# Attention scores with the opposite sign, and the masking of heads four to seven split around a scaling

## What is computed

```python
q = _l2norm(q) * q_scale; k = _l2norm(k) * k_scale        # per head, 8 heads of 128
sim = einsum('bhnid,bhnjd->bhnij', qb * 8.0, kw)          # 128 rows x 256 keys
sim = where(mask, sim, finfo.min)                         # causal, two tiles wide
attn = softmax(sim, axis=-1)
o = einsum('bhnij,bhnjd->bhnid', attn, vw) * gates
x = layernorm(x + o @ Wo.T)
```

## Time and profile before

| | |
|---|---|
| median of three runs | 1692.16 us (1691.88 to 1692.72) |
| the profiled execution | 1695.04 us |
| its span, from the first to the last instruction | 1693.3 us |
| TensorE busy | 1626.5 us, 96% |
| VectorE, ScalarE, GpSimd busy | 51%, 38%, 38% |
| steps of the attention | 32, about 33.2 us each |

### The profile page before, as it was taken

One profiled execution on the slowest core, in us unless ns is written; L12 is line 12 of the kernel. 1 busy time (PEld: TensorE's weight loads), 2 busy tenths in 40 slices (PEclk: granted clock), 3 DMA queues, 4 the chain that ended last, 5 costly groups with the idle time before them and its releaser, 6 DMA issues.

```text
span 1693.3 us, 30981 instructions
## 1 busy us (share of the span) xinstructions
PE 1626.5 (96%) x9466; PEld 1353.6 (80%) x9467; DVE 870.7 (51%) x2363; ACT 643.8 (38%) x1544; POOL 646.7 (38%) x724
## 2 busy tenths in 40 slices
PE   6899999999999999999999999898999999999886
PEld 4899899889988998998899899875677767777653
DVE  5445655655666556556556565565222222222787
ACT  4233433343344334333433433443233333333333
POOL 3222343243243333433432433433444444443443
PEclk9799999999999999999999999999999999999999
DMA  8010100010010001000000100357232333333785
GB/s 294 1 45 23 35 20 20 25 31 19 19 37 19 19 19 37 19 19 26 30 19 19 37 19 19 93 146 242 93 105 100 105 99 105 99 105 112 269 301 200
DMA packets 75099, 128.76 MB, mean 76 GB/s; under 512 B 9688, under 2 KB 26584, under 8 KB 75056
## 3 DMA queue, kind: packets, MB, share of 16 engines
q1 hardware_dynamic: 55584, 81.54, 14.5%
q0 software_dynamic: 13696, 38.24, 6.9%
q10 hardware_dynamic: 5776, 8.43, 1.8%
HBM read 88.98 MB, written 39.20 MB: 76 GB/s over the span
## 4 chain that ended last, share of the span: by engine, by line
PE 67%; issue 18%; DVE 5%; POOL 5%; DMA 2%; ACT 2%; POOLq 0%; another core or an unknown queue 0%; ACTq 0%; DVEq 0%; SPq 0%
PE bank L1110 23%; PE bank L1039 14%; PE bank L1066 9%; PE bank L1181 7%; PE bank L1200 5%; PE bank L1155 3%; POOL rnorm L655 2%; PE bank L1168 2%; PE bank L1013 2%; PE bank L1140 1%; PE bank L1049 1%; POOL ga L745 1%; DVE ssum L1342 1%; DMA bx<-x_d 1%; DVE qkn L1354 1%
## 5 line engine op out<-in xcount | busy, mean ns | idle before, releaser
L1110 PE MATMUL bank<-wh,xh 128*128 128x512 f32 (+2 forms) x896 | 339.7, 379 | 10.1 <-DVE qkn L1354 5.0
L1110 PE MATMUL bank<-wl,xh 128*128 128x512 f32 (+2 forms) x896 | 328.6, 367 | 0.0
L1110 PE MATMUL bank<-wh,xl 128*128 128x512 f32 (+2 forms) x896 | 327.8, 366 | 0.0
L655 POOL TENSOR_TENSOR rnorm<-ssmax,nhalf 128x4 f32<-128x4 f32 x128 | 133.8, 1045 | 426.6 <-DVE ssmax L1347 423.4
L1110 PEld LDWEIGHTS bank<-wh,xh 128*128 128x128 f32 x896 | 170.7, 191 | 43.0 <-DVE qkn L1354 16.4
L1110 PEld LDWEIGHTS bank<-wh,xl 128*128 128x128 f32 x896 | 170.3, 190 | 28.8
L1110 PEld LDWEIGHTS bank<-wl,xh 128*128 128x128 f32 x896 | 170.7, 191 | 22.7
L1333 DVE TENSOR_TENSOR bl<-bank,bh 128x512 fp32r<-128x512 f32 x104 | 71.7, 690 | 168.4 <-ACT bh L808 168.3
L1354 DVE TENSOR_TENSOR qkn<-bank,rnorm 128x512 f32<-128x512 f32 x128 | 88.5, 692 | 131.8 <-POOL rnorm L655 131.8
L1200 PE MATMUL bank<-woh,oh 128*128 128x256 f32 (+1 forms) x512 | 147.5, 288 | 1.0 <-DVE xr L1419 1.0
L1200 PE MATMUL bank<-wol,oh 128*128 128x256 f32 (+1 forms) x512 | 144.8, 283 | 0.0
(11 more groups left out here) (204 smaller groups left out, 3479.1 us busy)
## 6 DMA issues: line engine op xcount, KB each, us to landing
xt<-in_xT SPq DMA_DIRECT2D x33, 256.0 KB, 3.0
xr<-in_x SPq DMA_DIRECT2D x32, 256.0 KB, 2.6
x_d<-xr SPq DMA_DIRECT2D x32, 256.0 KB, 2.1
bx<-x_d SPq DMA_DIRECT2D x32, 256.0 KB, 4.9
ga<-eo_d SPq DMA_DIRECT2D x16, 512.0 KB, 4.9
gb<-eo_d SPq DMA_DIRECT2D x16, 512.0 KB, 6.5
out<-oo SPq DMA_DIRECT2D x32, 256.0 KB, 2.6
passing<-in_wqkvT SPq DMA_DIRECT2D x4, 1024.0 KB, 16.2
```

The costliest lines, as they stand in the source:

```text
L655: pool.tensor_tensor(rnorm[:, :], ssmax[:, :], nhalf[:, :], ALU.pow).then_inc(rn_s, 1)
L1110: mm = pe.matmul(b[:, 0:n], a[:, par, c, :], wt[:, c, cols], start=(c == 0 and k == 0), stop=(c == DC - 1 and k == 2))
```

## The change

The factor 8 on q becomes -8, so the scores have the opposite sign. The mask adds a large positive number in place of a large negative one, the masking instruction keeps the row minimum in place of the row maximum, and that minimum is the negated maximum of the true scores. So `mx`, `nmx`, the negating instruction, its wait and the semaphore `nmx_s` go; the exponential is taken of -1 times `pp` plus `neg_mx`, and waits for the maskings directly. In `step`, the two maskings of set 1 that read the first bank move ahead of `scale(s, 1, ...)`; the two of the second bank stay behind it. At the end of the attention, behind the loop, the two sets are masked whole as before.

```diff
-        mx = sbuf(sa, "mx", [P, H])
-        nmx = sbuf(sa, "nmx", [P, H])
+        neg_mx = sbuf(sa, "neg_mx", [P, 2 * H])
...
-            pool.affine_select(out=mask[:, 1, :], in_=mask[:, 1, :], compare_op=ALU.is_ge, fill=-BIG, base=0,
+            pool.affine_select(out=mask[:, 1, :], in_=mask[:, 1, :], compare_op=ALU.is_ge, fill=BIG, base=0,
...
             def exps(u, g):
-                act.wait_ge(nmx_s, 2 * u + g + 1)
+                act.wait_ge(masked, 8 * u + 4 * g + 4)
                 for h in range(g * HPG, (g + 1) * HPG):
-                    ins = act.activation(pp[:, h, :], pp[:, h, :], ACT.Exp, bias=nmx[:, h:h + 1],
+                    ins = act.activation(pp[:, h, :], pp[:, h, :], ACT.Exp, bias=neg_mx[:, h:h + 1], scale=-1.0,
                                          accum_out=esum[:, h:h + 1])
...
-            dve.scalar_tensor_tensor(out=qks[:, :], in0=qks[:, :], scalar=8.0, in1=ksc[:, :],
+            dve.scalar_tensor_tensor(out=qks[:, :], in0=qks[:, :], scalar=-8.0, in1=ksc[:, :],
...
-            def mask_max(u, g, upar, first):
-                for b in range(2):
+            def mask_max(u, g, upar, first, banks=range(2)):
+                for b in banks:
...
-                            mask[:, 1 - upar:3 - upar, :].rearrange("p k j -> p (k j)"), 1.0, -3e38, ALU.add, ALU.max,
-                            mx[:, h:h + 1]).then_inc(masked, 1)
-                dve.wait_ge(masked, 8 * u + 4 * g + 4)
-                dve.tensor_scalar(nmx[:, g * HPG:(g + 1) * HPG], mx[:, g * HPG:(g + 1) * HPG], -1.0, None, ALU.mult)\
-                   .then_inc(nmx_s, 1)
+                            mask[:, 1 - upar:3 - upar, :].rearrange("p k j -> p (k j)"), 1.0, 3e38, ALU.add, ALU.min,
+                            neg_mx[:, h:h + 1]).then_inc(masked, 1)
...
                 if attn_on:
                     gate_scale(u, 0, u_first)
+                    mask_max(u, 1, 1 - par, u_first, (0,))
                 scale(s, 1, attn_on)
                 if attn_on:
-                    mask_max(u, 1, 1 - par, u_first)
+                    mask_max(u, 1, 1 - par, u_first, (1,))
```

More of the change, by code:

```diff
@@ L246, in block_kernel @@
         masked = sem("masked")
-        nmx_s = sem("nmx_s")
         exp_s = sem("exp_s")
@@ L589, in _ @@
                                pattern=[[-1, P]], channel_multiplier=1).then_inc(consts, 1)
-            pool.affine_select(out=mask[:, 1, :], in_=mask[:, 1, :], compare_op=ALU.is_ge, fill=-BIG, base=0,
+            pool.affine_select(out=mask[:, 1, :], in_=mask[:, 1, :], compare_op=ALU.is_ge, fill=BIG, base=0,
                                pattern=[[-1, P]], channel_multiplier=1).then_inc(consts, 1)
-            pool.affine_select(out=mask[:, 0, :], in_=mask[:, 0, :], compare_op=ALU.is_ge, fill=-BIG, base=0,
+            pool.affine_select(out=mask[:, 0, :], in_=mask[:, 0, :], compare_op=ALU.is_ge, fill=BIG, base=0,
                                pattern=[[1, P]], channel_multiplier=-1).then_inc(consts, 1)
             for i in range(0, NT // 2, BLOCKS // 2):
-                pool.memset(flag[:, i:i + 1], -BIG).then_inc(consts, 1)
+                pool.memset(flag[:, i:i + 1], BIG).then_inc(consts, 1)
             def group_constants():
```

## The result

The changed kernel took 1683.74 us (median of five, 1678.3 to 1685.15) against 1692.16 us (five runs, 1690.74 to 1693.98): 8.4 us less by the medians, inside the range; 11.7 were forecast. The ratio on record is 0.9936, with a 95% interval of 0.992 to 0.9952, or 8.1 to 13.5 us. On a second chip the same two kernels stood at 1680.57 and 1693.11, a ratio of 0.9919 (0.9899 to 0.9939), 12.5 us less.

A forecast was written before the change was run, and what follows sets the result against it. TensorE's waits for VectorE in the attention were taken as the bound. Gains of 4.7 (set 1's scores), 6.6 (v0) and 0.4 (end) sum to 11.7 us, predicting 1680.5 us, range 1677.7 to 1687.3.

The forecast's parts named there:

- What bounds the kernel: In the attention, VectorE savings count only where TensorE waits: set 1's scores lose 0.18 us a step, v0 0.27 or 0.35.
- The negation of set 0 goes: Ahead of `heads_low`: removal makes `kTl` earlier, so set 1's scores gain 0.18 us over 26 loop steps, 4.7 us.
- so the whole 0.18 comes back: Set 1's scores: `kTl` ends an unbroken VectorE run, so removing set 0's negation recovers all 0.18 us a step.
- 0.12 needed: How much earlier `kTl` must come after k0's start, 2.70 instead of 2.82 us, for set 1's scores not to wait.
- at least the 0.17: Least VectorE time in us that removing set 0's negation, ahead of `heads_low`, gives; perhaps 0.3 with its wait.
- The negation of set 1 goes, and half of the maskings move: Reduce behind q1's squares starts earlier, so v0 gains 0.18 us in 15 even steps, 0.26 in 15 odd: 6.6 us.
- What the move costs: Two maskings fill the hole before k0's scaling, about 0.7 us; its lead over k1 stays near 0.44, no new wait.
- The sign: Minimum for maximum, the fill, -8 and the exponential's scale of -1 change only constants in instructions that stay: cost 0.
- The end of the attention: Behind the loop, two more negations disappear from a VectorE that TensorE waits for: 0.4 us.
- Only v0 gains: Rival: set 1's scores wait for something beside `kTl`, so only 7.0 us is gained, 1685.2 us; chance 0.14.
- No gain: Rival: TensorE's own work sets its pace, or another link fills the gap; time stays 1692 us; chance 0.08.
- Maskings held by GpSimd: Rival: GpSimd's product shuts out the moved pair, delaying k0's scaling and k1; +48 us, 1740 us; chance 0.04.

The follow-up runs named there:

- the two idle instructions: Changed kernel plus a wait and unused multiplication where the negation of set 0 stood, 1685.32 us, or where that of set 1 stood, 1679.05 us.
- the two second profiles: Kernel before and changed kernel, each profiled again without edits: one time of 1689.26 us before, median 1680.57 us changed.
- the two spread kernels: Changed kernel and kernel before, each with ScalarE's weight loads at the start of the experts' part spread out: 1676.77 and 1688.75 us.

## Why the prediction was right, and where its numbers were off

**What bounds the kernel** was right. TensorE's waits in the attention were two places of 0.18 and 0.27 to 0.35 behind a busy share of 99.8%, and the two idle instructions show that VectorE's time counts only where TensorE's wait ends on it: 0.38 a pass ahead of `kTl`, nothing behind set 1, once VectorE is ahead of the squares there.

**The negation of set 0 goes.** The mechanism was right, the term mis-sized: 4.7 us forecast. Measured, the even steps gained 0.18 and the odd ones 0.10, 13 of each, 3.6 us. (The first pass of the loop gained less, and the written-out steps 3 and 5, counted as nothing, gained 0.14 and 0.06; the sum stays the same.) The step that failed is "so the whole 0.18 comes back", in two of its parts. The "0.12 needed" came from a written-out step, where the weight load follows `kTl` by 0.06; in the loop it follows by 0.13, and more than 0.12 was needed. The even steps, where `kTl` came 0.28 earlier, had it to spare. And the odd steps did not get the "at least the 0.17": the negation held VectorE for 0.21 there, but its work starts 0.12 later than before, so `kTl` came only 0.10 earlier. Why it starts later is open.

**The negation of set 1 goes, and half of the maskings move.** 6.6 us forecast. The reduce starts 0.03 behind its squares, and the loop's steps gained 0.19 and 0.27. The four written-out steps 2 to 5 had stalls of 0.34 to 0.37, and lost them whole (0.80 and 0.81 after, the unhindered 0.80), so they gave 1.4 where the formula counts 0.9. Together 13 x 0.19 + 13 x 0.27 + 1.4 = 7.4. The forecast that the negation alone does nearly all of it was right: the move was given 1.4 us and is worth 0.17 us, in step 3, on top of it.

**What the move costs** was right: a pair of 0.70, the lead of k0's scaling 0.42 against 0.44, and no wait of k1 (q1 and k1 together 5.57 as before). **The sign** cost nothing: a masking 0.42, an exponential 0.50 as before. The Trainium skill, "ScalarE: Activation LUTs" (What ACT_TABLE_LOAD costs), charges extra for operands read through a pointer and nothing for an immediate scale. The trace agrees, with these 0.50.

**The end of the attention** gave 0.24 (from the last v0 to the experts' first matmul, 27.24 before and 27.00 after), where 0.4 was forecast.

**The sum.** 3.6 + 7.4 + 0.2 = 11.2 by the steps' own differences, 11.8 to 12.0 by the two first traces, in which the late step at 310 stood against the kernel before; 11.7 was forecast. In the two second profiles, without such a step, the stretch from step 2's v0 to the last v0 is 10.8 shorter, and step 2 and the end add 0.5. That 11.2 lies so close to 11.7 is in part luck: the first term was 1.1 too high and the second 0.8 too low. The 8.4 of the first medians is less than that; by the second chip's medians it is 12.5, and by the two spread kernels 12.0. "The experts' part changes nothing; it begins earlier" fits these two. In the first pair of traces the wait for rows took 2.5 more, and it varies by chance between executions; that this is also what the first medians lack is likely and not shown. In the range, the upper bounds of the three terms add up to 5.6 + 9.3 + 0.4 = 15.3, not to about 14.5; the measured time is not near that end.

**The rivals.** Only v0 gains: refuted by k0 to q1, 4.30 and 4.37, though its reason, that the written-out step may differ by its form, was right for 0.07. No gain: refuted. Maskings held by GpSimd: the moved pair, at 629.92, beside the power (from 629.52) and up to the product's start at 630.50, kept its 0.42. What the row 1.29 in the earlier trace rows showed of some instructions appeared once more in an experiment: the idle multiplication behind set 1 took 0.40 in place of 0.17. It ended at 630.93, and GpSimd's product at 630.90. That fits the rule of the Trainium skill, "SBUF — State Buffer" (SBUF: two separate sides), by which a masking with one input in SBUF passes, and a multiplication within SBUF, which can take a two-port mode, is held until GpSimd's instruction is over.

**A better version.** The changed kernel with the spread loads has the lowest median, 1676.77 us, though its interval overlaps with those of the changed kernel. The move could probably be left out of it, by the run without it; that combination was not run.

Open: what sets the length of the rows' load, and why VectorE's work ahead of `kTl` starts 0.12 later in odd steps.

## What to carry to other kernels

A busy share near 100% is no proof that an engine loses nothing. Compare the start-to-start time of a block that may wait with the same block where it can't, and count the difference over the steps. An instruction of 0.17 us on an engine that is idle 40% of the time can cost its whole length, or nothing: it depends on whether the bound engine waits for what stands behind it. Take the block that can't wait from the same form of code: here a written-out step and a loop step differed by 0.07 us. Two edits that clear the same wait are worth it once; run each alone before adding them up. And where the time of a later stage varies from run to run, read the gain at the end of the stage that was edited.

## What was not expected

The time from the last v0 to the end varied by 8.2 us over ten profiles, at the same work. In the odd steps of the loop the hole in front of the first masking grew from 0.12 to 0.24 us, though nothing was added ahead of it; with an idle instruction put in elsewhere it was 0.12 again, and the same delay stood further ahead. And the weight load that waits for `kTl` starts 0.12 or 0.13 behind it in the loop, 0.05 or 0.06 in the written-out steps.
